# Row sums of the diagonal's odd key tiles on TensorE in every quad

## What is computed

```python
def reference(x, Wq, Wk, Wv, Wo, weight, bias, ln_gamma, ln_beta):
    xn = _layernorm(x)                      # x: (2, 2048, 512)
    q = (xn @ Wq).reshape(B, T, H, Dh)      # H = 16, Dh = 32; k, v likewise
    scores = jnp.einsum('bthd,bshd->bhts', q, k)
    mask = jnp.tril(jnp.ones((T, T)))
    attn = jax.nn.softmax(scores * mask / T ** 0.5, axis=-1)
    s = jnp.einsum('bhts,bshd->bthd', attn, v).reshape(B, T, H * Dh) @ Wo
    g = _silu(layernorm(xn, ln_gamma, ln_beta) @ ternary_quantize(weight).T + bias)
    return x + s * g
```

## Time and profile before

| | |
|---|---|
| median of 3 runs | 1556.85 us (1556.77 to 1557.6) |
| the profiled execution | 1554.97 us |
| its span in the trace | 1553.2 us |
| granted TensorE clock, mean | 0.987 of 2.4 GHz |
| busy: TensorE | 1495.3 us, 96% |
| busy: weight loads | 904.9 us, 58% |
| busy: VectorE | 1053.1 us, 68% |
| busy: GpSimd | 871.1 us, 56% |
| busy: ScalarE | 774.7 us, 50% |

### The profile page before, as it was taken

One profiled execution on the slowest core, in us unless ns is written; L12 is line 12 of the kernel. 1 busy time (PEld: TensorE's weight loads), 2 busy tenths in 40 slices (PEclk: granted clock), 3 DMA queues, 4 the chain that ended last, 5 costly groups with the idle time before them and its releaser, 6 DMA issues.

```text
span 1553.2 us, 24547 instructions
## 1 busy us (share of the span) xinstructions
PE 1495.3 (96%) x8554; PEld 904.9 (58%) x8554; DVE 1053.1 (68%) x2389; ACT 774.7 (50%) x1614; POOL 871.1 (56%) x723
## 2 busy tenths in 40 slices
PE   6999999999999999999999999999999999998877
PEld 5888888887444555455454554555555555544655
DVE  7545656643787777777777777777777777752566
ACT  4333322332555666665656666665666665665110
POOL 4100000000666877877778777787777877679341
PEclk9999999999899999999999999999999999999988
DMA  6668866548851442324145145142324511313998
GB/s 209 189 178 229 259 190 177 164 135 232 197 130 36 83 109 63 80 69 113 36 110 130 36 89 123 50 95 68 93 52 92 130 36 39 96 40 86 323 343 277
DMA packets 110426, 201.42 MB, mean 130 GB/s; under 512 B 14688, under 2 KB 32736, under 8 KB 109280
## 3 DMA queue, kind: packets, MB, share of 16 engines
q1 hardware_dynamic: 99216, 177.86, 43.0%
q10 hardware_dynamic: 11088, 22.02, 4.3%
HBM read 123.22 MB, written 76.28 MB: 128 GB/s over the span
## 4 chain that ended last, share of the span: by engine, by line
PE 81%; DVE 6%; DMA 4%; POOL 3%; ACT 3%; issue 1%; SPq 1%; ACTq 0%; POOLq 0%; DVEq 0%
PE psP L1287 21%; PE psS L1365 17%; PE psO L1388 16%; PE psM L1265 16%; PE psL L1394 6%; DMA gr<-gate 3%; DVE psM L1073 2%; POOL acc L814 2%; PE psT L1212 2%; PE psL L1403 2%; DVE mx L1076 1%; ACT Pb L937 1%; ACT acc L937 1%; POOL Pb L797 1%; DVE oo L1200 1%
## 5 line engine op out<-in xcount | busy, mean ns | idle before, releaser
L814 POOL TENSOR_TENSOR acc<-acc,Pb 128x1024 f32<-128x1024 f32 (+2 forms) x308 | 600.2, 1977 | 159.3 <-PE psO L1388 128.6
L937 ACT ACTIVATE Pb<-psS 128x512 f32<-128x512 f32 (+2 forms) x1122 | 518.2, 533 | 296.6 <-PE psS L1365 288.6
L1076 DVE TENSOR_REDUCE mx<-psM 128x1 f32<-128x512 f32 x768 | 484.9, 683 | 158.8 <-PE psM L1265 157.6
L1365 PE MATMUL psS<-half 97*128 97x512 f32 (+1 forms) x1247 | 473.9, 397 | 7.0 <-ACT Pb L937 4.6
L1265 PE MATMUL psM<-half 96*128 96x512 f32 (+3 forms) x1280 | 457.9, 383 | 6.6 <-DVE mx L1073 3.1
L1365 PEld LDWEIGHTS psS<-half 97*128 97x128 f32 x1247 | 234.4, 190 | 245.5 <-issue 105.3
L1265 PEld LDWEIGHTS psM<-half 96*128 96x128 f32 x1280 | 235.7, 190 | 77.1 <-DVE mx L1076 26.3
L1073 DVE CUSTOM_DVE_ANT_0 psM<-psM,negm 128x256 f32<-128x256 f32 (+3 forms) x512 | 238.2, 517 | 62.1 <-PE psM L1265 61.9
L1388 PE MATMUL psO<-Pb,Vs 128*32 128x512 f32 (+3 forms) x2304 | 267.6, 534 | 0.9 <-POOL Pb L797 0.9
L797 POOL TENSOR_SCALAR_AFFINE_SELECT Pb<-Pb 128x256 f32<-128x256 f32 x240 | 93.9, 406 | 81.0 <-ACT Pb L937 78.9
L1394 PE MATMUL psL<-Pb,ones 128*32 128x512 f32 (+3 forms) x1072 | 125.6, 537 | 0.0
(11 more groups left out here) (101 smaller groups left out, 1479.5 us busy)
## 6 DMA issues: line engine op xcount, KB each, us to landing
half<-q_hi SPq DMA_DIRECT2D x32, 512.0 KB, 10.4
half<-k_hi SPq DMA_DIRECT2D x32, 512.0 KB, 10.5
xt<-in_L_attn_x SPq DMA_DIRECT2D x8, 1024.0 KB, 7.9
q_hi<-st_hi SPq DMA_DIRECT2D x32, 256.0 KB, 4.4
q_lo<-st_lo SPq DMA_DIRECT2D x32, 256.0 KB, 4.8
gate<-gs SPq DMA_DIRECT2D x32, 256.0 KB, 2.2
k_hi<-st_hi SPq DMA_DIRECT2D x32, 256.0 KB, 2.8
k_lo<-st_lo SPq DMA_DIRECT2D x32, 256.0 KB, 2.9
```

Of the source, the lines that this page charges most:

```text
L814: g.tensor_tensor(to[:, :, o:], to[:, :, o:], Pb[s % RING][:, heads, o:], ALU.add).then_inc(sum_done, 1)
L937: a.activation(weights(s, h)[:, o:], score_bank(s * HQ + h, last)[:, o:], ACT.Exp, scale=SCALE).then_inc(exp_done, 1)
L1076: ins = v.tensor_reduce(flat[:, heads, slots], bank[:, 0:ns * w].rearrange("p (a b c) -> p a b c", a=nh, c=w), AX.X, ALU.max)
L1365: t.matmul(score_bank(n, last)[:, o:], Ks[par][j // HALF][0:MROW + 1, h, j % HALF * P:(j % HALF + 1) * P], Qs[par][c // 2][0:MROW + 1, h, ...
```

## The change

Before, the two diagonal groups of chunks 1, 2 and 3 go past GpSimd's adds in the last quad only. After, they do in every quad: `summed` loses its argument `last`, the thresholds of sum_done count NSUM = 14 adds of groups in a quad instead of 20, and everything else keeps its place. Chunk 0 is as before.

```diff
-def summed(gr, last):
+def summed(gr):
 
     c, j = GROUPS[gr]
-    return not (last and c > 0 and j >= CT * c)
+    return c == 0 or j < CT * c
...
+NSUM = summed_before(NG)
...
# GpSimd, add:
                         if j > 0:
-                            pool.wait_ge(sum_done, START + (qn * NG + summed_before(gr, not more)) * NPAIR + p - 1)
+                            pool.wait_ge(sum_done, START + (qn * NSUM + summed_before(gr)) * NPAIR + p - 1)
...
# GpSimd, the loop over groups:
                         select(s)
                         select(s + 1)
-                        if j > CT * c and summed(gr, not more):
+                        if j > CT * c and summed(gr):
                             add(gr - 1)
                             add(gr)
...
# ScalarE, exps:
                     if s % 2:
-                        act.wait_ge(sum_done, START + (qn * NG + summed_before(max(0, s // 2 - 1), last) - (s < 2)) * NPAIR)
+                        act.wait_ge(sum_done, START + (qn * NSUM + summed_before(max(0, s // 2 - 1)) - (s < 2)) * NPAIR)
...
# TensorE, values and row_sums:
-                    if j > 0 and j % 2 == 0 or not summed(s // 2, not more):
+                    if j > 0 and j % 2 == 0 or not summed(s // 2):
...
-                    pe.wait_ge(sum_done, START + (qn * NG + summed_before(last, final)) * NPAIR)
+                    pe.wait_ge(sum_done, START + (qn * NSUM + summed_before(last)) * NPAIR)
```

More of the change, by code:

```diff
@@ L95, in diagonals_before, with summed_before @@
     return sum(on_diagonal(i) for i in range(s))
-def summed(gr, last):
+def summed(gr):
     c, j = GROUPS[gr]
-    return not (last and c > 0 and j >= CT * c)
-def summed_before(gr, last):
-    return sum(summed(g, last) for g in range(gr))
+    return c == 0 or j < CT * c
+def summed_before(gr):
+    return sum(summed(g) for g in range(gr))
+NSUM = summed_before(NG)
 OWN_STEPS = 19
@@ L1396, in values, with row_sums @@
                     ins.then_inc(pv_done, 1)
-                def row_sums(qn, c, final):
+                def row_sums(qn, c):
                     last = FIRST[c + 1] if c + 1 < NCH else NG
-                    pe.wait_ge(sum_done, START + (qn * NG + summed_before(last, final)) * NPAIR)
+                    pe.wait_ge(sum_done, START + (qn * NSUM + summed_before(last)) * NPAIR)
                     for h in range(HQ):
@@ L1433, in quad @@
                     if j == 0 and (c > 0 or follows):
-                        row_sums(*((qn, c - 1, not more) if c else (qn - 1, NCH - 1, False)))
+                        row_sums(*((qn, c - 1) if c else (qn - 1, NCH - 1)))
                     if not on_diagonal(s):
@@ L1438, in quad @@
                 if not more:
-                    row_sums(qn, NCH - 1, True)
+                    row_sums(qn, NCH - 1)
             quads(quad)
```

## The result

The changed kernel takes 1569.04 us (median of 4 runs, 1566.75 to 1570.06), the kernel before 1556.81 us beside it (4 runs, 1556.28 to 1557.6): a ratio of 1.0076 with a 95% interval of 1.0059 to 1.0094. It is slower, by 0.76%. One execution of the kernel before among the 22 beside the last three experiments took 2796.55 us and is left out of the ratios; nothing in the runs explains it. The profiled execution took 1568.86 us, 1567.1 us of it span, 13.9 us more than before.

A forecast was written before the change was run, and what follows sets the result against it. The prediction took TensorE to bound the kernel: 18.3 us of added row sums less 4.0 us of waiting for GpSimd gave +14.3 us, so 1571.2 us from a median of 1556.85 us, range 1567 to 1575 us.

The forecast's parts named there:

- The bound: Whole kernel: TensorE is busy 96% of the span and carries 81% of the chain, GpSimd 56% and 3%.
- The two prices: At 21 chunk ends, TensorE's new row sums: 384-column (wide) set 0.65 us, 128-column (narrow) set 0.22 us, together 18.3 us.
- I take no cover: At all 21 chunk ends, no part of TensorE's added 18.3 us was expected to be hidden.
- The sum: Whole kernel: +18.3 - 4.0 = +14.3 us, profiled run 1569.3 us, median 1571.2 us, 0.92% slower.
- The check of chunk 1 as a whole: Chunk 1, quad 7 against quad 1: 28.32 against 28.09 us, net +0.23 us, where the terms give +0.20.
- The removed adds: Behind chunk 1 in quads 1 to 6, ScalarE's wait for GpSimd's adds goes: 6 x 0.67 = 4.0 us saved.
- Smaller sum waits: Lower sum_done thresholds for TensorE's row sums and ScalarE's odd steps: cost nothing and bring nothing.
- Headroom: Rival: TensorE's new row sums fit beside weight loads and exponentials, leaving only the 4.0 us gain, 1552.8 us; 2%.
- Partly covered: Rival: sums of chunks 2 and 3 use TensorE's idle 1.26 us in quads 1 to 6, saving 7.6 us, 1563.6 us; 7%.
- No relief: Rival: another wait replaces chunk 1's wait for GpSimd, or quad 0's clock dips differently; without the gain 1575.1 us; 9%.
- The change doesn't reach the quads: Rival: the edit has no effect in the quads, time stays 1556.9 us; 1%.
- What would show it: Profile after: 192 row-sum instructions of each shape, 16 GpSimd adds of each, quads 1 to 6 longer by 1.9 to 2.0 us.

The follow-up runs named there:

- e_c1: Against the kernel before, TensorE takes the row sums of the diagonal's odd tiles in chunk 1 only; 1558.52 us, attention +1.6 us.
- null run: The kernel before run against itself as if it were a change, nothing edited; 1553.99 us against 1554.52, ratio 0.9997.
- e_both: Against the kernel before, TensorE's row sums put in as in the changed kernel, but GpSimd's adds stay too; 1569.2 us, attention 1047.1 us.
- e_none: Against the kernel before, GpSimd's adds removed in quads 0 to 6 and no row sums put on TensorE; 1550.68 us, attention -3.6 us.
- e_wide: Against the kernel before, only the 384-column tiles go to TensorE, GpSimd keeps adding the 128-column ones; 1562.26 us, attention +9.7 us.
- e_narrow: Against the kernel before, only the 128-column tiles go to TensorE, GpSimd keeps adding the 384-column ones; 1560.23 us, attention +4.4 us.
- a_again: The changed kernel run once more against the kernel before; 1567.67 us, ratio 1.0079, attention +12.1 us.
- b_move: Against the kernel before, GpSimd's masked-key block of chunk 1 moved between the diagonal's wide and narrow adds, sums unchanged; 1549.2 us, ratio 0.9954.
- b_move2: Kernel before with GpSimd's masked-key block moved between chunk 1's wide and narrow adds, plus quad 7's chunks 1 and 2 back on GpSimd; 1549.99 us, ratio 0.9961.

## Why the prediction was right, and where its reasoning was not

**The bound.** Right: TensorE carried the chain, and what was put on it came out in the span. **The two prices**, read as the difference of quad 7 and quad 1, were exact: 0.65 and 0.22 us, again at chunks 2 and 3 and in quad 0, which quad 7 couldn't show. "I take no cover" held at all 21 chunk ends of the changed kernel. VectorE's numerators wait 0.22 us longer for their signal, as said (0.78 instead of 0.56 us at chunk 1 of quad 1), which shows as no cost beyond the set's own. From the intervals the sets come to 18.2 us.

**The sum.** 14.3 us stood in it, 14.06 us were measured in the attention and 13.9 in the span; the profiled run was put at 1569.3 us and took 1568.86. The check of chunk 1 as a whole (+0.23) came out in e_c1 as +0.21 to +0.26 in five quads. The median was put 2.2 us too high, mostly by one step: the 1.9 us by which before's median stood over its profiled execution were carried over to the changed kernel, whose median stands 0.2 us over its own. That offset is not a property of the kernel: in the null run, which is the same kernel, the median lies 0.9 us below the profiled execution. One more slip does not touch the forecast: the range of 1567 to 1575 us is said to take in the case without relief, but that case's own sum, 1575.1 us, lies just outside.

**The removed adds.** The amount was right; the reason given is one of two, and the terms are not independent. The prediction booked -4.0 us to the removal of GpSimd's adds, as a term beside the +18.3. e_both keeps the adds and still has 0.57 to 0.64 us of relief in each of quads 1 to 6. The exponentials of step 13 wait for the later of two paths, and the wide set of 0.65 us stands on one of them, in front of it; it fills a gap that was 0.62 us wide (577.02 against 576.40). So there are two true statements about the same 4 us: the adds' removal alone brings it (e_none, -3.64), and once the row sums are on TensorE the removal brings next to nothing (1047.11 against 1046.57). The weak step is to read "in quad 7, where the adds are gone, they start without a wait" as the adds' doing alone: quad 7 also had the wide set, and its row could not tell one from the other. For the change as it was made the sum is right, since quad 7 has both halves of it. For half of the change it need not be: the same terms give the relief of e_none rightly and put e_both 3.7 us too high.

**Smaller sum waits** cost nothing, as said; no interval but those named moved by more than a few hundredths in quads 1 to 6.

**The rivals.** *Headroom* is refuted. By the row weight loads are busy for 65.81 of 128 us, and the same stretch after reads

```profile
542.00:670.00 128.00, 127.39 (x836) 66.59 (x828) 94.81 (x238) 78.28 (x172) 85.25 (x71) 1.00 0.35 84
```

with TensorE idle for 0.61 us of 128 instead of 1.26 and weight loads still at 52%. Each set was nevertheless paid in full, alone (e_wide, e_narrow) and together. By the Trainium skill, Perfetto Trace Analysis, section "Identifying the Most-Contended Engine", TensorE's headroom is to be judged by the share of weight loads and by the matmul work done against the peak (MFU), which was not worked out here. These runs disagree with reading room from the share of weight loads, at least for matmuls of fp32 operands with 32 output partitions. *Partly covered* would have left the idle 1.26 us to be used at chunks 2 and 3. Half of it did go, but that half is the wait of 0.64 us at chunk 1 that had been counted; chunks 2 and 3 paid 0.87 us each. *No relief* didn't happen. The part of it on the clock did, in a_again (last section). *The change doesn't reach the quads* fell with the counts of 192.

**What would show it.** The signs named came: 192 instructions of each shape, 16 adds of each, 104.6 us less GpSimd, 1.92 us from step 12 to 13, the wait for the adds gone, 0.65 us more idling ahead of first exponentials. The quads grew by 1.78 to 2.00 us for 1.9 to 2.0 announced; quad 5, whose wait was the longest, is the one below.

**What stays open.** The traces give 14.06 and 12.1 us for the attention, the medians 12.2 and 11.9 for the whole. The 1.5 us of the low clock in quad 0 (last section) would fill most of that gap if the timed runs of the changed kernel mostly lacked it, but they have no trace of their own, so this is not shown. For b_move it is the other way round: -4.2 us in the traces, -6.6 and -4.4 by the medians. What the first of these has beyond the mechanism is not explained.

## What to carry to other kernels

Price an added piece of work on the busiest engine by a place in the same trace that already has it, and count it in full until a place shows cover. A wait that ends late and work that is put ahead of it are not two terms but two paths into one start: write both arrival times down and take the later, before and after, or the gain of removing the wait is booked twice or to the wrong edit. When an engine with room to spare holds up the busiest one, look first at what stands ahead of the late work in its own queue: moving that block (b_move) brought the 4 us for which this change paid 18.

## What the runs showed of the hardware

**A stretch of low clock that comes and goes.** Quad 0 has between 470 and 480 us a spell in which TensorE's granted clock is 0.83 on average in the kernel before, in the null execution of the same kernel, and in the changed kernel; ten of the twelve traces have it. In a second execution of the changed kernel it isn't there. The stretches (us, busy PE, PEld, DVE, ACT, POOL, clock, DMA, GB/s) of after and then of a_again:

```profile
470.00:480.00 10.00, 9.31 (x46) 3.81 (x45) 6.77 (x30) 3.12 (x6) 4.56 (x4) 0.83 0.00 1
```

```profile
470.00:480.00 10.00, 9.21 (x50) 4.60 (x50) 8.40 (x33) 4.25 (x10) 5.48 (x4) 1.00 0.00 1
```

A mean of 0.83 is a third of the 10 us at 1.2 GHz and the rest at 2.4. Where it is missing, the interval from step 20 to step 21 is 1.51 us shorter than before, and that is most of the difference between a_again's +12.1 and +14.06. The prediction had put it at 10 x 0.17 = 1.7 us. In b_move2 it wasn't at this place either, but an earlier and longer one was:

```profile
425.00:445.00 20.00, 19.06 (x83) 10.18 (x79) 13.23 (x39) 7.76 (x19) 10.29 (x13) 0.74 0.41 97
```

There the intervals of chunk 1's last steps are 3.6 us longer, and the quad 0.87 us longer on balance. TensorE was 93 to 95% busy in the stretches with the low clock and 92% in the one without, and what decides when the clock falls none of the runs tells. It means that a comparison by the trace of an edit worth less than some 2 us has to leave quad 0 out, as the six equal quads allow.

**The rest of the program** took 520.1 to 522.7 us in ten of the twelve traces, and 518.3 (e_wide) and 526.7 (b_move2) in the other two, none of which these edits touch. The clock varies in the output stage too: from 1490 to 1510 us it was 0.83 in the kernel before and 0.98 in the null execution of the same kernel. That is why the attention, and not the span, is compared above.

**GpSimd's load did not press on the others.** With 105 us of its adds gone, VectorE's reductions of the maxima take 684 ns each instead of 683 and ScalarE is busy for 774.6 us instead of 774.7. And e_none, with the same adds gone and nothing added, was shorter at the waits for them and nowhere else. So in this kernel an add on GpSimd showed no cost to the others but its place in the queue.
